# Finer stack transfers and a new unit order in two attentions, and an earlier release of the first mixes in a recurrence

## The reference, cut to what matters

```
ln = layernorm(x);      q, k, v = split(ln @ w_qkv + b_qkv)
x  = x + merge(softmax(q k^T / sqrt(32) masked) v) @ w_ao + b_ao       # 16 heads of 32
ln = layernorm(x);      q = ln @ w_q;  k, v = split(ctx @ w_kv)
x  = x + merge(softmax(...) v) @ w_co + b_co
x  = x + gelu(layernorm(x) @ w1) @ w2

xa = ln(x);  sx = shift(xa) - xa
t  = tanh((xa + sx * maa_x) @ maa_w1)              # 5 groups of 32: w, k, v, r, g
m_j = t_j @ maa_w2[j];   x_j = xa + sx * (maa_j + m_j)
w = exp(-exp(time_decay + tanh(x_w @ decay_w1) @ decay_w2))
r, k, v = x_r @ Wr.T, x_k @ Wk.T, x_v @ Wv.T;  g = silu(x_g @ Wg.T)
s_new = k v + w * s;  out = r (faaaa * k v + s)    # token by token, 32 heads of 16
x = x + groupnorm(out) * g @ Wo.T;   then a gated feed-forward part
```

## Time and profile before

| | us |
|---|---|
| median of 3 runs (3984.1 to 3984.75) | 3984.41 |
| the profiled execution's own time | 3986.14 |
| its span | 3984.4 |
| attentions, from the first to the last score matmul | 31.4 to 1495.2 |
| a load of x (512 KB), from issue to landing, median | 3.5 |
| recurrence, from its first matmul of `t` to the end | 2274 to 3984 |

### The profile page before, as it was taken

How to read it: one execution, slowest core, us unless ns; L and a number is a source line. 1 busy time by engine, 2 the same in 40 slices (tenths; PEclk the granted TensorE clock), 3 DMA queues, 4 the chain that set the end, 5 groups by cost and what they waited for, 6 DMA issues and landing times. The chain is left out here.

```text
span 3984.4 us, 71128 instructions
## 1 busy us (share of the span) xinstructions
PE 3665.5 (92%) x21676; PEld 2809.6 (71%) x21676; DVE 2992.5 (75%) x6738; ACT 2030.6 (51%) x5166; POOL 1829.6 (46%) x1256
## 2 busy tenths in 40 slices
PE   7998999999999988999999878999999999999976
PEld 6777777778777777999999755666666666666643
DVE  6778777888888885665556557888888888888883
ACT  5777777777777775555455322333333333333321
POOL 5444444544444441000000036776777777777761
PEclk9999999999999998999999988999999999999988
DMA  5344443544444442000110300000000000000000
GB/s 152 95 105 111 109 102 95 149 116 126 121 124 111 112 133 98 32 32 32 33 46 32 108 28 20 25 25 25 25 25 25 25 25 25 25 25 25 19 19 16
DMA packets 143809, 256.54 MB, mean 64 GB/s; under 512 B 24384, under 2 KB 29248, under 8 KB 142624
## 3 DMA queue, kind: packets, MB, share of 16 engines
q1 hardware_dynamic: 143648, 254.48, 23.3%
HBM read 107.61 MB, written 33.55 MB: 35 GB/s over the span
## 5 line engine op out<-in xcount | busy, mean ns | idle before, releaser
L463 POOL TENSOR_TENSOR a_prob<-a_prob,a_rsums 128x512 f32<-128x512 f32 x512 | 541.6, 1060 | 780.9 <-DVE a_rsums L645 780.7
L1446 POOL TENSOR_TENSOR c_S<-c_S,c_rT 128x1024 f32<-128x1024 f32 x256 | 603.2, 2358 | 364.0 <-DVE c_S L1801 364.0
L535 ACT ACTIVATE a_prob<-a_t,a_tmin 128x256 f32<-128x256 f32 x1024 | 512.7, 501 | 363.8 <-DVE a_tmin L638 362.8
L1801 DVE TENSOR_TENSOR_SCAN c_S<-c_wT,c_vb 128x512 f32<-128x512 f32 x512 | 624.8, 1220 | 50.5 <-issue 8.6
L1796 DVE TENSOR_TENSOR c_vb<-c_kT,c_vb 128x510 f32<-128x510 f32 x512 | 350.8, 685 | 214.1 <-PE c_vb L2010 194.9
L634 DVE SCALAR_TENSOR_TENSOR a_ps_s<-a_ps_s,a_mask 128x512 f32<-128x512 f32 x512 | 357.2, 698 | 172.1 <-PE a_ps_s L741 103.6
L638 DVE CUSTOM_DVE_ANT_0 a_t<-a_ps_s,a_mneg 128x256 f32<-128x256 f32 x1024 | 394.1, 422 | 60.0 <-issue 0.7
L751 PE MATMUL a_ps_t<-w_ident,a_prob 128*128 128x128 f32 x2048 | 324.1, 282 | 27.2 <-ACT a_probT L545 17.5
L2010 PE MATMUL c_vb<-c_vhl,c_spread 128*128 128x512 f32 x512 | 283.1, 572 | 54.1 <-DVE c_S L1801 38.1
L741 PE MATMUL a_ps_s<-a_stack 96*128 96x256 f32 x1024 | 230.7, 308 | 82.6 <-DMA a_stack<-a_parts_qk 64.2
L545 ACT COPY a_probT<-a_ps_t 128x512 f32<-128x512 f32 x512 | 288.2, 563 | 1.6 <-PE a_ps_t L751 1.6
(11 more groups left out here) (255 smaller groups left out, 10080.9 us busy)
## 6 DMA issues: line engine op xcount, KB each, us to landing
a_stack<-a_parts_qk SPq DMA_DIRECT2D x768, 128.0 KB, 2.4
x<-w_x_out SPq DMA_DIRECT2D x48, 512.0 KB, 2.8
w_x_in<-x SPq DMA_DIRECT2D x48, 512.0 KB, 3.9
w_x_out<-x SPq DMA_DIRECT2D x32, 512.0 KB, 3.5
w_x_in<-in_x SPq DMA_DIRECT2D x16, 512.0 KB, 3.5
w_x_out<-in_x SPq DMA_DIRECT2D x16, 512.0 KB, 3.5
a_enc<-in_ctx SPq DMA_DIRECT2D x16, 512.0 KB, 4.4
b_xb<-x SPq DMA_DIRECT2D x16, 512.0 KB, 4.2
```

The source lines that it names most:

```text
L463: nc.gpsimd.tensor_tensor(prob[:, h % 4, :, :], prob[:, h % 4, :, :], rsums[:, h, :].unsqueeze(2).to_broadcast([P, TC, T]), ALU.mult).then ...
L535: op = nc.scalar.activation(prob[:, n % 4, tc, :], t[:, n % 2, tc, :], ACT.Exp, bias=tmin[:, n, tc:tc + 1], scale=-1.0, accum_out=psums[:, ...
L1446: nc.gpsimd.tensor_tensor(S[:, n % 4, :, :], S[:, n % 4, :, :], rT[:, par, :, :], ALU.mult).then_inc(z_ready, 1)
L1801: nc.vector.tensor_tensor_scan(flat(pair(S[:, n % 4, :, :], i)), flat(pair(wT[:, par, :, :], i)), flat(x), 0.0, ALU.mult, ALU.add).then_in ...
```

## The change

In the attentions the order of the units is another, the bias row is added to `xb` at head 2 and not at head 1, and the first pair is no longer moved as one. Chunk 0 is moved once `k0` is split, ahead of the load of `xb` on SP's queue, chunk 1 once `k1` is split, behind that load. Each chunk takes 12 transfers of half the size (rows of 1 KB in place of 2 KB), so an iteration issues 36 stack transfers in place of 24. PE waits for them by chunk: at heads 0 to 3, 4 to 7, and 8 to 11 (for the second pair), and at no other head. In the recurrence a new semaphore, `wk_ready`, counts the second tanh (group k). `mw0` waits for it; the wait for all five tanh goes to `mr0`.

```diff
-    FILLS = {0: ["q3"], 1: ["k2"], 2: ["k3"], 3: ["ctx2"], 4: ["ctx3", "v0"], 5: ["v1"], 6: ["out0", "encT0"], 7: ["lnT0", "lnT1"], 8: ["encT1"], 9: ["out1", "q0"], 10: ["k0"], 11: ["ctx0", "q1"], 12: ["k1"], 13: ["q2"], 14: ["ctx1"]}
-    AT = {"xb": 1, "root": 4, "stats": 4, "apply": 6}
+    FILLS = {0: ["q3"], 1: ["ctx2"], 2: ["k2"], 3: ["k3"], 4: ["ctx3"], 5: ["v0", "v1"], 6: ["encT0", "out0"], 7: ["lnT0", "lnT1"], 8: ["encT1", "out1"], 9: ["ctx0", "q0"], 10: ["k0"], 11: ["q1"], 12: ["k1"], 13: ["ctx1"], 14: ["q2"]}
+    AT = {"xb": 2, "root": 4, "stats": 4, "apply": 6}
...
-                def stack_up(split, pair):
+                def stack_up(split, pair, chunks, done):
                     sp.wait_ge(qk_split, split)
                     for g in range(HPC):
                         for slot, pick in enumerate(SLOTS):
                             sp.dma_start(
-                                stack[slot * HD:(slot + 1) * HD, :, g, 2 * pair:2 * pair + 2, :]
-                                .rearrange("p s i t -> p s (i t)").bitcast(F32),
-                                parts_qk[g * HD:(g + 1) * HD, pair, pick, :, :]
-                                .rearrange("p s i t -> p s (i t)").bitcast(F32)).then_inc(stacked[g], 16)
-                def first_pair(k):
-                    stack_up((k + 1) * 2 * KC + (QK.index("k1") + 1 - LATE - 2 * KC), 0)
+                                stack[slot * HD:(slot + 1) * HD, :, g, 2 * pair:2 * pair + 2, :][:, :, chunks, :].bitcast(F32),
+                                parts_qk[g * HD:(g + 1) * HD, pair, pick, chunks, :].bitcast(F32)).then_inc(done[g], 16)
+                def first_pair(k, i):
+                    stack_up((k + 1) * 2 * KC + (QK.index(f"k{i}") + 1 - LATE - 2 * KC), 0, slice(i, i + 1), stacked[f"chunk{i}"])
...
                 with sp.Fori(1, B - 1) as k:
                     load_front(k + 1, SELF)
                     second_pair(k)
                     store(k - 1, SELF)
+                    first_pair(k + 1, 0)
                     load_xb(k, SELF)
-                    first_pair(k + 1)
+                    first_pair(k + 1, 1)
...
-                            if m % 2 == 0:
-                                pe.wait_ge(stacked[g], 16 * 3 * (k * 2 + (m // 2 + 1)))
+                            if m < 3:
+                                pe.wait_ge(stacked[("chunk0", "chunk1", "pair1")[m]][g], 48 * (k + 1))
...
                             op = nc.scalar.activation(tT[row:row + DM, place, :], ..., ACT.Tanh)
+                            if n == "k":
+                                op.then_inc(wk_ready, 1)
                         op.then_inc(done, 1)
...
                 def fill_together(k, name, second):
+                    if name == "mr0":
+                        pe.wait_ge(emptied["act"], units_0.emptied(k + 2, "Xt") if first(k) else units.emptied(k + 1, "t"))
                     if name == "mw0":
-                        pe.wait_ge(emptied["act"], units_0.emptied(k + 2, "Xt") if first(k) else units.emptied(k + 1, "t"))
+                        pe.wait_ge(wk_ready, k + 2)
```

More of the change, by code:

```diff
@@ L215, in attentions @@
         high_ready, ln_split, qk_split = sem("high_ready"), sem("ln_split"), sem("qk_split")
-        stacked = [sem(f"stacked_{g}") for g in range(HPC)]
+        stacked = {what: [sem(f"stacked_{what}_{g}") for g in range(HPC)] for what in ("chunk0", "chunk1", "pair1")}
         s_filled, t_ready = sem("s_filled"), sem("t_ready")
@@ L328, in stack_up @@
                             sp.dma_start(
-                                stack[slot * HD:(slot + 1) * HD, :, g, 2 * pair:2 * pair + 2, :]
-                                .rearrange("p s i t -> p s (i t)").bitcast(F32),
-                                parts_qk[g * HD:(g + 1) * HD, pair, pick, :, :]
-                                .rearrange("p s i t -> p s (i t)").bitcast(F32)).then_inc(stacked[g], 16)
-                def first_pair(k):
-                    stack_up((k + 1) * 2 * KC + (QK.index("k1") + 1 - LATE - 2 * KC), 0)
+                                stack[slot * HD:(slot + 1) * HD, :, g, 2 * pair:2 * pair + 2, :][:, :, chunks, :].bitcast(F32),
+                                parts_qk[g * HD:(g + 1) * HD, pair, pick, chunks, :].bitcast(F32)).then_inc(done[g], 16)
+                def first_pair(k, i):
+                    stack_up((k + 1) * 2 * KC + (QK.index(f"k{i}") + 1 - LATE - 2 * KC), 0, slice(i, i + 1), stacked[f"chunk{i}"])
                 def second_pair(k):
-                    stack_up((k + 1) * 2 * KC, 1)
+                    stack_up((k + 1) * 2 * KC, 1, slice(0, 2), stacked["pair1"])
                 def load_x(k, phase, buffer, loaded):
@@ L383, in load_half @@
                                  ).then_inc(half_loaded[at % 3], 16)
-                first_pair(0)
+                first_pair(0, 0)
+                first_pair(0, 1)
                 load_front(1, SELF)
@@ L391, in _ @@
                 load_half("q", 0)
-                first_pair(1)
+                first_pair(1, 0)
+                first_pair(1, 1)
                 with sp.Fori(1, B - 1) as k:
@@ L405, in _ @@
                 store(B - 2, SELF)
+                first_pair(B, 0)
                 load_xb(B - 1, SELF)
-                first_pair(B)
+                first_pair(B, 1)
                 load_half("o", 0)
@@ L413, in _ @@
                 store(B - 1, SELF)
+                first_pair(B + 1, 0)
                 load_xb(B, CROSS)
-                first_pair(B + 1)
+                first_pair(B + 1, 1)
                 with sp.Fori(B + 1, 2 * B - 1) as k:
@@ L1219, in phase_c @@
         th_ready, g_used = sem("th_ready"), sem("g_used")
+        wk_ready = sem("wk_ready")
         w_ready, vb_filled, scanned = sem("w_ready"), sem("vb_filled"), sem("scanned")
```

## The result

3950.12 us (median of 4 runs, 3948.45 to 3952.59) against 3984.4 before: ratio 0.9914, 95% interval 0.9897 to 0.9932. The change gains 34 us; I forecast 92, and a range that ended at 3945. The profiled execution has a span of 3947.9, 36.5 less than the one before. Where these came from is read from starts in both traces. From the first tanh of the recurrence to the end, 1704.2 became 1670.2: 34.0 less. From DVE's first mask product of iteration 0 to that of iteration 31 of the attentions, 1421.4 became 1421.7: nothing gained. The rest, 2.8, lies between the two parts and at the start.

The account below looks back on a forecast made before the run. PE was taken to bound the recurrence; DVE, PE and the layernorm chain each a section of the attentions. Recurrence 57 us plus attentions 35 made 92, off a span of 3984.4: forecast 3892 us, range 3855 to 3945.

Parts of the forecast that it names:

- Tanh, 16 us: Recurrence: first mixes need two tanh of five, so PE starts 1.15 us earlier, 14 times: 16 us.
- Clock, 3.3 of 4.1 x 14 = 57 us: Recurrence: the lower-clock stretch behind the 1.58 us stop goes, 3.3 a body; with tanh, less DVE's 0.35, 4.1 x 14.
- Head 9 to head 0, 16.6: Attentions, DVE's section: `out1` fills a wait of about 0.45 at head 10; 16.6 us in place of 17.06.
- Head 0 to head 7, 20.0: Attentions, PE's section: the stack is no longer waited for at head 0; 20.0 us against 20.40.
- The POOL stop of 1.25 at head 4: Attentions: PE waits 1.25 us at head 4 for POOL's product behind the moved bias row, replacing the stack's wait.
- Cross iterations, 0.8 less: Attentions: each cross iteration gains 0.3 + 0.4 and a little of the clock's falls, 0.8 us.
- rival (4): SP's queue: issues with 1 KB rows cost over 0.64 us, x comes late, kernel slower; 4128 at 0.96 each; chance 0.05.
- The wait of 1.2 us for x: Attentions: DVE waits 1.2 us for the next sample's x at head 4, hidden in slack of 1.3 before head 6.
- Rival (1): Recurrence: the clock's falls stay, 46 us gained in place of 92: 3938; chance 0.16.
- Rival (2): Attentions gain nothing, the ring of DVE and POOL holds their pace; 57 us gained: 3927; chance 0.12.
- Both together: Clock's falls stay in the recurrence and the attentions gain nothing: 3973; chance 0.04.
- rival (5): Recurrence: the change does not do what it says, `mw0` waits at its bank or weights: 3949; chance 0.04.

Follow-up runs that it names:

- e9: Changed kernel with four recurrence bodies in each turn of the loop in place of two (SP's loop stays at two): 3941.7 us, ratio 0.9891.
- e13: Changed kernel with the twelve looped bodies of the recurrence written out, so no engine jumps back there: 3927.7 us, ratio 0.9855.
- e16: Kernel before the change, with all looped bodies of both parts written out: 3971.8 us, ratio 0.9969.
- e17: Changed kernel with all looped bodies of both parts written out (SP's own loop stays): 3904.7 us, ratio 0.9801.
- e4: Changed kernel with `q2` at head 13 and `ctx1` at head 14, so the last move before the turn has no drain: 3940.5 us, ratio 0.9884.
- e2: Changed kernel with the old order of units and old place of the bias row, keeping chunked transfers and the recurrence part: 3948.3 us, ratio 0.9906.
- e7: Changed kernel with the bias row back ahead of head 0's product on POOL: 3960.1 us, ratio 0.9937.
- e6: Changed kernel with the cross q weights' second half loaded ahead of the second pair's transfers at the last self iteration: 3949.5 us, ratio 0.9906.
- e18: e17 with SP's loop written out too and x loaded ahead of the first pair's 24 issues: 3899.5 us, ratio 0.9785.
- e14: Changed kernel with the 28 looped bodies of the attentions written out (SP's own loop stays): 3912.3 us, ratio 0.9809.
- e10: Changed kernel with two attention bodies in each turn of their loops in place of one (SP's loop as before): 3991.8 us, ratio 1.0015.
- e1: Kernel before with only the recurrence part of the change (`wk_ready`), attentions as before: 3955.1 us, ratio 0.9916.

## Why the prediction was wrong, step by step

**Tanh, 16 us: right in size, not everywhere.** The stop is 0.46 where I had 0.43 left. In the five bodies behind the jump another stop takes its place, so these give nothing back: 99.4 to 99.9 us after the change, 99.1 in most of them before.

**Clock, 3.3 of 4.1 x 14 = 57 us: the step that failed is "I expect it gone, since only 0.43 us of idling are left", with 0.35 as all that DVE takes back.** It holds in the eight bodies away from the jump: 99.1 became 95.1, 4.0 for the 4.1 forecast. In the five behind the jump DVE stands 3.3 to 3.7 us, at least 2.6 more than in the other bodies, PE stops 1.7 to 2.1 for it, and the fall stays: 5 x 4.4 = 22 us, nearly the 23 by which 34 falls short of 57. The idle times of 2.02 and 1.38 stood in DVE's timeline before, in every second body. I had read one body, and not the one behind the jump. e9 and e13 take the turns away and the slow bodies go with them; e16 to e17 gives 51 of the 57. The size was near: in e13 a fall of 6.8 us makes a body 97.9 in place of 95.0, 2.9 where I had 3.3.

The rule that I weighed there (the Trainium skill, TensorE: Matmul & The Clock Gate, "Why this matters for your kernels", a long pause is needed) doesn't agree with these traces: e13 has falls that begin 2.3 to 2.5 us behind stops of 0.58 us.

That the stops behind a jump are there because DVE's next instructions have to be brought in is argued, not shown. What speaks for it is that they come and go with the packets of the instruction queue: three packets and two stops behind each jump of the recurrence, none of either at the start of the body beside it, and no packet in the attention loop with one body a turn. The Trainium skill (Advanced Engine Details and Errata, "ISA Cache") gives an engine other than TensorE two cache lines of 256 instructions. The counts of the traces don't settle it: a turn of one attention body has 202 recorded DVE instructions and shows 0.7 us of idle, one of two bodies has 399 and shows 4.2 to 5.2, one of two recurrence bodies has 478 and shows 3.3 to 3.7, and 399 and 478 are fewer than the page's two lines hold. The page's branch of 51 to 108 ns ("Control Flow Timing") would not explain any of them.

**Head 9 to head 0, 16.6: failed.** It takes 17.40. "The new order has the same moves" was true of the moves and not of their places. I took 0.45 off for the wait at head 10; 0.16 came (16.90 in e4, where `out1` now waits 0.21 itself). And `q2` became the last move before the turn. That costs 0.5 us in each of the fourteen self iterations, which `ctx1` without a drain had covered; e4 shows it. In this loop no instructions are brought in, so these 0.5 us are another cost of the turn than the stops in the recurrence, and what makes them is open.

**Head 0 to head 7, 20.0: near in size (20.26), wrong in reason.** I gave the section to PE from head 0 on. DVE has it up to head 4: in e2 the stack's wait vanishes and the section stays (20.47 to 20.43). The POOL stop of 1.25 at head 4 isn't there, since PE already stands 1.09 us at head 0 and 0.70 at head 2. The old place of the bias row costs 0.5 us in the new order (e7); my sum had priced only the new place.

**Cross iterations, 0.8 less: failed.** Five of twelve take 45.7, 0.45 less than before. Seven have a fall at head 1 or 2 and take 47.0. What a fall costs depends on its place, which I had not looked at. Before, ten of the twelve had one at head 15 and took as long as the two without (46.1 to 46.2), except one. In e4 three have one at head 15 alone and take 45.86 as those without; the one with a fall at head 1 takes 47.16. I had priced the disappearance of falls, and neither their place nor that they could come up elsewhere.

**The one iteration with the weights: not priced.** It cost 3.5 us; e6 shows the place. I counted every transfer of the moved steps in the loop, and none in the iterations beside it.

**SP: right.** An issue takes 0.64 us, so rival (4) had no price at that size. The wait of 1.2 us for x in each iteration, which I had forecast and called hidden, did not come: DVE waits for x 6 times, 7.9 us in all. The halved transfers land in 2.0 us where the whole ones take 2.4 (medians), a little sooner, where I had let landing stay. But the place of rival (4) was real: as soon as DVE gains 0.5 us at the turn, it waits for x (16.0 us in 15 iterations in e4, 48 in 29 in e17); e18 shows that this wait lies in DVE's slack in front of head 6, as I had argued.

**The rivals.** Rival (1) held in five bodies of thirteen. Rival (2) held in the total of the attentions (0 of 35), though as a balance of 5.2 won and 6.3 lost and some change at the ends. Both together were 3973. The measured 3950 is my sum with 34 of 57 and 0 of 35. That rival (5) names 3949 is luck: it has the recurrence give nothing, and the recurrence gave all.

**Open.** Why the same body, with the same stops, has a fall of 3.4 us in one execution and none in the next (e6, e13). Why the stop behind the recurrence's jump is 0.5 to 0.9 us in e14, with the same recurrence, in place of 1.8; the trace shows two packets of queue 14 there in place of three, and DVE's first stop without the second, behind each of the five jumps, but not what makes it two. And what bounds the attentions' 43.7 us in e18; a third buffer for PE's transposes was not tried.

## What to carry to other kernels

Before pricing the removal of a wait, read the other engines at that very place, in the iteration right behind the loop's jump too. Idle time there marked "issue" costs nothing while someone else waits, and it is what stands on the path once that wait is gone. When units change places, look at which one now stands last before the turn, and at the odd iterations at the ends of the loops. A gain of some us through the clock needs every stop near it gone, not only the longest. And a fall is priced by where it lies: in these cross iterations one of 3.4 us cost nothing at head 15 and 1.3 us at head 1.

## What the runs showed of the hardware that I had not expected

- A loop's turn costs DVE 0.5 us behind a drain with 202 recorded instructions in the body (self iterations). The stops behind it are 4.2 to 5.2 us with 399 (e10), 3.3 to 3.7 with 478, and 3.4 and 3.6 with 954 (e9). Written out, the attentions of the changed kernel lose 33 us (1421.7 to 1388.6).
- These stops come with packets of the instruction queue: behind each jump of the recurrence three packets and two stops (before, after, e1), two packets and one stop (e10, e14); with four bodies in a turn seven packets and two stops (e9). With one attention body in a turn there are none. Straight code has four to six packets an iteration and no such stop (e14).
- With the attentions written out, a head of the same DVE work takes 2.27 us in place of 2.34.
- The lower clock came in stretches of 3.4 or 6.8 us in most bodies and iterations, of 10.2 in a body of the kernel before (100.7). One of 3.4 costs 1.2 to 1.3 us in the self iterations, at head 1 or 2 of the cross ones and in the recurrence, and nothing at head 15 of the cross iterations. In the recurrence one of 6.8 costs 2.9, and 4.4 with the stop of 1.8 ahead of it.
- Halving a transfer inside SBUF to 64 KB leaves its issue at 0.64 us and brings its landing from 2.4 to 2.0.
